# Attention loop ordered by a table of places, scores from 16-bit high and low halves

## The chip, the cores and the metric

One core of a Trainium2 chip runs the kernel. The number that counts is the device time of one execution in microseconds. The kernel before was timed three times: 1871.81, 1875.1 and 1884.6 us, median 1875.1.

## The reference, cut to what matters

The input is 16 images of 3 x 256 x 256. A template correlation turns each image into 256 tokens of 256 numbers; then come one attention block and one gated feed-forward block, each followed by a layer normalisation. The change lies in the attention block (and in the last microseconds of the token stage, where its weights are prepared):

```python
x = rmsnorm(tokens, norm_w)                    # tokens 256 x 256 per image
q = (x @ Wq)  -> 16 heads of 64 ; k, v = x @ Wkv -> 8 heads of 64
q, k = l2norm over 64, times (gamma + 1) * 8
sim = q k^T                                    # two query heads share one key head
sim = 50 * tanh(sim / 50) * 64 ** -0.5, causal mask, softmax
out = (sum over the two query heads of attn v) @ Wout
h = layernorm(tokens + out)
```

## The kernel before, in words

The program has three stages, one block after the other, with a barrier between them: the token stage (correlation, lines 123 to 591), the attention stage (694 to 1142) and the feed-forward stage (1167 to 1501). All orders are written by hand; each engine runs its own list strictly in order and waits on semaphores. Nothing is scheduled by a compiler.

**Attention stage.** The 16 images go in 4 groups of 4. Each engine emits a `FIRST` stretch (image 0 is prepared), a loop of three `BODY` stretches (one group each, and meanwhile the next group's tokens and first image are prepared) and a `FINAL` stretch (the last group). A stretch is a list of steps made by `first_order` and `attention_order`, and every engine walks the same list and issues its part of each step. The steps:

- `turn_h`: transposes of the normalised tokens `hn` on TensorE, split by ScalarE and VectorE into `ht_hi` and `ht_lo`.
- `make` 0 to 7: projection to q, k, v of one image, six matmuls of 512 columns per bank; ScalarE copies the bank to `raw` or `v`. After each third it also squares `raw` (L900). `make` 8 to 14: four transposes of the scaled `raw`; ScalarE copies queries to `qt` (L904), VectorE multiplies keys by the folded gamma into `kt` (L988).
- `sum`, `root`, `scale`: VectorE's l2 norm of q and k.
- `score` n (n = 0 to 31 in a group: image times key head): four float32 matmuls on 64 rows each, two of 256 and two of 128 columns, where the pair m = 0, 1 uses the lower and the upper 64 rows (L1102); then ScalarE's tanh (L911) and exp (L914) and GpSimd's causal mask (L838).
- `mix` n: six float32 matmuls of 65 columns (L1116), two heads behind `score` n; VectorE divides by the sum (L995, L998, L1002).
- `turn_o`, `project`: output transposes (L1125, copied by ScalarE at L921) and the projection with `w_out` (L1137), one `project` series of 64 matmul passes at the end of a group; VectorE adds it to `h` and takes the statistics.
- `rms_sum`, `rms_root`, `rms_scale`: the next group's tokens `hn` are squared and summed by ScalarE (L872), rooted by GpSimd (L829, L831), scaled by VectorE (L941). `rms_sum` stands behind score 17 of the group.

Three PSUM banks (`BANKS`) serve all of `turn_h`, `make`, `turn_o` and `project` in rotation: a step waits until the one three places earlier has been read out; the first of a stretch waits until all of the stretch before are (L1056). Scores have two buffers, `mixed` has one.

**The load of the next group's tokens.** SyncE's list for a group is: wait until all bank jobs of the stretch before are done, load `hn` (L785), then words and `h`, and at the end of the group wait for the normalised `h` (`s_x1`, set by VectorE's L1034) and store it (L805). So the load of `hn` for the next group stands behind the store of the group before.

## Time and profile before

| | |
|---|---|
| median of 3 runs | 1875.1 us (1871.81 to 1884.6) |
| the profiled execution, its own time | 1875.0 us |
| its span, first to last instruction | 1873.3 us |
| token stage | 0 to 523.5 us |
| attention: preparation and first group | 523.5 to 721.6 us |
| attention: second, third group | 721.6 to 885.4, 885.4 to 1049.1 us |
| attention: last group | 1049.1 to 1198.6 us |
| feed-forward stage | 1198.6 to 1873.3 us |
| mean granted TensorE clock | 0.980 of full |

The borders of groups are the first score matmul behind a projection. TensorE is at work 95% of the span, VectorE 59%, ScalarE 47%, GpSimd 23%. A duration of a single matmul in the trace holds the length of the pipe; what a matmul costs in a row of them is the distance from start to start.

### The profile page before, as it was taken

The numbers are of one execution on the slowest core, as the hardware profiler recorded it, in microseconds if no ns is written. First come the engines' busy times: TensorE is split into PE (matmuls) and PEld (weight loads), VectorE is DVE, ScalarE is ACT, GpSimd is POOL, SyncE is SP. The second block draws the span as 40 slices with busy tenths as digits, with TensorE's granted clock in tenths as the row PEclk, the third lists the DMA queues.
The fourth block names the chain that finished last, engine by engine and source line by source line (L and its number), as shares of the span: only waits on it lengthen the run. The fifth ranks groups of instructions, "written<-read, shape, count | busy, mean of one in ns | idle before, by whom it ended". The sixth has DMA issues, their size and how long they took to land. (4 is left out here: it accounts for less than half of the span.)

```text
span 1873.3 us, 31348 instructions
## 1 busy us (share of the span) xinstructions
PE 1781.0 (95%) x11640; PEld 1548.6 (83%) x11640; DVE 1104.9 (59%) x1964; ACT 873.9 (47%) x1077; POOL 429.0 (23%) x516
## 2 busy tenths in 40 slices
PE   5999999999969999999999999799999999999998
PEld 5999999999958877877787788688888888888886
DVE  9899898998756665565666656334141432415142
ACT  6555566665437764684676477122222222222221
POOL 2000000000212221211222123143343434434342
PEclk9999999999979999999999999799999999999999
DMA  5323212224010002000200102240000000000000
GB/s 175 120 90 124 82 74 83 82 78 155 23 70 34 24 17 85 24 16 10 92 24 17 61 25 95 72 153 23 0 24 1 23 24 1 23 1 23 1 12 12
DMA packets 26363, 97.11 MB, mean 52 GB/s; under 512 B 3033, under 2 KB 11353, under 8 KB 20962
## 3 DMA queue, kind: packets, MB, share of 16 engines
q1 hardware_dynamic: 26210, 94.96, 14.7%
q8 instruction: 110, 1.80, 0.4%
q14 instruction: 43, 0.35, 0.1%
HBM read 82.33 MB, written 24.15 MB: 57 GB/s over the span
## 5 line engine op out<-in xcount | busy, mean ns | idle before, releaser
L569 PE MATMUL conv<-w_hi,x_hi 128*128 128x368 f16 (+5 forms) x1320 | 353.0, 278 | 3.5 <-issue 3.5
L569 PE MATMUL conv<-w_lo,x_hi 128*128 128x368 f16 (+5 forms) x1320 | 353.8, 278 | 0.0
L569 PE MATMUL conv<-w_hi,x_lo 128*128 128x368 f16 (+5 forms) x1320 | 352.6, 278 | 0.0
L1328 ACT ACTIVATE raw_c<-ring,sh 128x512 f32<-128x512 f32 x128 | 87.5, 689 | 334.4 <-PE ring L1431 334.3
L838 POOL TENSOR_SCALAR_AFFINE_SELECT probs<-probs 128x256 f32<-128x256 f32 x256 | 124.4, 509 | 430.7 <-ACT probs L914 430.7
L1116 PE MATMUL mixed<-v,probs 128*128 128x65 f32 x1536 | 199.2, 280 | 14.7 <-DVE o L998 11.9
L1116 PEld LDWEIGHTS mixed<-v,probs 128*128 128x128 f32 x1536 | 182.9, 193 | 31.2 <-issue 16.0
L1287 POOL TENSOR_TENSOR ha_lo<-raw_c,ha_hi 128x512 fp32r<-128x512 f32 x128 | 165.3, 1291 | 189.3 <-DVE ha_hi L1340 189.3
L1340 DVE CAST ha_hi<-raw_c 128x512 fp32r<-128x512 f32 x128 | 86.3, 674 | 201.0 <-ACT raw_c L1328 198.8
L569 PEld LDWEIGHTS conv<-w_hi,x_hi 128*128 128x128 f16 x1320 | 192.3, 146 | 12.4 <-issue 4.0
L569 PEld LDWEIGHTS conv<-w_lo,x_hi 128*128 128x128 f16 x1320 | 192.6, 146 | 8.1
L1431 PE MATMUL ring<-ha_hi,wh 128*128 128x512 f32 x512 | 199.2, 389 | 0.0
L1431 PE MATMUL ring<-ha_lo,wh 128*128 128x512 f32 x512 | 199.2, 389 | 0.0
L1431 PE MATMUL ring<-hb_lo,wh 128*128 128x512 f32 x512 | 199.2, 389 | 0.0
L1431 PE MATMUL ring<-hb_hi,wh 128*128 128x512 f32 x512 | 199.2, 389 | 0.0
L569 PEld LDWEIGHTS conv<-w_hi,x_lo 128*128 128x128 f16 x1320 | 192.0, 145 | 7.5
L911 ACT ACTIVATE probs<-sim 128x768 f32<-128x768 f32 x128 | 103.8, 811 | 99.3 <-PE sim L1102 97.8
L1340 DVE CAST hb_hi<-raw_c 128x512 fp32r<-128x512 f32 x64 | 35.8, 559 | 187.7 <-ACT raw_c L1328 187.3
L326 ACT ACTIVATE lines<-turn 128x512 f32<-128x512 f32 x96 | 50.0, 606 | 172.1 <-PE turn L550 172.1
L1102 PE MATMUL sim<-qt,kt 64*128 64x256 f32 (+1 forms) x1024 | 120.0, 354 | 3.2 <-DVE kt L988 2.8
L1102 PEld LDWEIGHTS sim<-qt,kt 64*128 64x128 f32 x1024 | 89.9, 189 | 39.9 <-issue 33.0
L412 DVE TENSOR_TENSOR_SCAN box<-lines 128x271 f32<-128x271 f32 x192 | 120.1, 699 | 3.9 <-ACT lines L326 3.9
(148 smaller groups left out, 3443.4 us busy)
## 6 DMA issues: line engine op xcount, KB each, us to landing
xt<-x_columns_in SPq DMA_DIRECT2D x12, 1163.0 KB, 6.0
xp<-x_patches_in SPq DMA_DIRECT2D x12, 1152.0 KB, 5.1
hidden_words<-hidden_weights_in SPq DMA_DIRECT2D x8, 1408.0 KB, 8.0
words<-hidden_words SPq DMA_DIRECT2D x32, 352.0 KB, 3.1
wh<-hidden_words SPq DMA_DIRECT2D x8, 1024.0 KB, 10.0
tokens<-planes SPq DMA_DIRECT2D x4, 1024.0 KB, 4.6
lines<-tokens SPq DMA_DIRECT2D x4, 1024.0 KB, 5.6
h<-tokens SPq DMA_DIRECT2D x4, 1024.0 KB, 6.9
```

The source lines that it names most:

```text
L326: act.activation(dst, turn[:, k % 4], ACT.Copy).then_inc(s_across, 1)
L412: return dve.tensor_tensor_scan(out, line[:, TH:TH + SCAN], line[:, 0:SCAN], 0.0, ALU.add, ALU.subtract)
L569: ins = pe.matmul(out, xs[:, c, RI - 1 - i:RI - 1 - i + NR, :, x].rearrange("p r g -> p (r g)"), w, start=(t == 0), stop=(t == len(terms) ...
L838: ins = pool.affine_select(out=diag, in_=diag, compare_op=ALU.is_ge, fill=0.0, base=0, pattern=[[0, 2], [1, P]], channel_multiplier=-1)
L911: act.activation(probs[:, n % 4], sim[:, n % 2, :, 0:3 * P], ACT.Tanh, scale=1.0 / CLAMP).then_inc(s_tanh, 1)
L1102: ins = pe.matmul(sim[:, n % 2, m, 2 * P * jb:2 * P * jb + P * (2 - jb)], kt[rows, img % 2, hd, P * jb:P * jb + P], qt[rows, img % 2, hd, ...
L1116: ins = pe.matmul(out, probs[:, n % 4, m, at:at + P], v[:, img % 2, jb, 2 * (hd // 2) + m], start=(jb == 0), stop=(jb == ib), skip_group_c ...
L1287: pool.tensor_tensor(dst[1][:, u % KH], raw[:, u % 4], dst[0][:, u % KH].bitcast(F32), ALU.subtract).then_inc(s_lo, 1)
L1328: act.activation(raw[:, u % 4], bank, ACT.Gelu, scale=scale[:, m:m + 1]).then_inc(s_gelu, 1)
L1340: dve.tensor_copy(dst[0][:, u % KH], raw[:, u % 4]).then_inc(s_hi, 1)
L1431: ins = pe.matmul(bank, a, b, start=start, stop=False, skip_group_check=True)
```

## The change

**Places.** Each step gets a number of its own, in units of heads (`IMAGE_AT` for images 1 to 3 of a group, `EDGE_AT` for the next group's image 0, `GROUP_AT` for the steps of a group), and the list of a stretch is the steps sorted by it. The squaring becomes a step (`square`), the transposes are now `turn`, and `rms_sum` falls into four pieces of two squares each, written to a buffer of their own (`dump`). Sorted, three of the four pieces of `rms_sum` (places -28.062, -15.449, -0.477) come ahead of score 0 (place 0), which opened the list before, and ahead of the group's first `make`. The three banks stay.

**Scores.** q times the folded gamma is kept as a float16 high part (ScalarE, four activations of 128 columns with a scale read per partition) and a float16 rest (VectorE, four scalar_tensor_tensor); keys likewise, times 8, without gamma, once per pair of key heads (one activation, one scalar_tensor_tensor). A score is 12 float16 matmuls, three terms (hi hi, lo hi, hi lo) of what were 4 float32 ones. The gamma is brought into the range of float16 by a maximum over all partitions: GpSimd's `partition_all_reduce` at the end of its list in the token stage, and four small VectorE instructions behind it (`fold_span`), ahead of the stage's last `scale`. The tanh takes its scale from an SBUF column.

```diff
             split_weights()
+            pool.wait_ge(sh.s_gamma, 6)
+            pool.partition_all_reduce(sh.span[:, 1:2], sh.span[:, 0:1], P, bass.bass_isa.ReduceOp.max)\
+                .then_inc(sh.s_span, 1)
...
+            def fold_span():
+                dve.wait_ge(sh.s_span, 1)
+                dve.tensor_scalar(sh.span[:, 2:3], sh.span[:, 1:2], 1.0 / GAMMA_SPAN, 1.0, ALU.mult, ALU.max)\
...
                     scale_tokens()
+                    fold_span()
                 scale(g, c, n, 3)
...
-SLOTS = (
...
+IMAGE_AT = {
+    ("make", 1): -8, ("make", 2): -8, ("make", 0): -7.681, ("square", 0): -7.022, ("sum", 0): -6.626,
...
+GROUP_AT = {
+    ("rms_sum", 0): -28.062, ("rms_sum", 1): -15.449, ("rms_sum", 2): -0.477, ("rms_sum", 3): 15.005,
...
+    at += [(t, step) for step, t in GROUP_AT.items() if not last or step[0] == "project"]
+    return [step for t, step in sorted(at)]
...
                         act.wait_ge(s_hn, n * 16 + 16)
-                        if run.before:
-
-                            act.wait_ge(s_ss, image(g, RMS_AT // HEADS + 1) * 2 + 2)
-                        for a in range(PR):
-                            ins = act.activation(squares[:, a * D:(a + 1) * D], hn[:, a], ACT.Square,
-                                                 accum_out=ss[:, a:a + 1])
-                        ins.then_inc(s_hsum, 1)
+                        for a in range(2 * step[1], 2 * step[1] + 2):
+                            ins = act.activation(dump[:, a], hn[:, a], ACT.Square, accum_out=ss[:, a:a + 1])
+                        if step[1] == 3:
+                            ins.then_inc(s_hsum, 1)
...
+                        if r < 2:
+                            for e in range(4):
+                                u = 4 * r + e
+                                ins = act.activation(q_hi[:, img % 2, u, cols], bank[:, e * P:(e + 1) * P], ACT.Copy,
+                                                     scale=gamma[:, u:u + 1])
+                            ins.then_inc(s_qkhi, 1)
+                        else:
+                            act.activation(k_hi[:, img % 2, :, cols], bank.rearrange("p (h t) -> p h t", t=P),
+                                           ACT.Copy, scale=KEY_SCALE).then_inc(s_qkhi, 1)
...
-                                       scale=1.0 / CLAMP).then_inc(s_tanh, 1)
+                                       scale=sh.span[:, 2:3]).then_inc(s_tanh, 1)
...
+                                ins = dve.scalar_tensor_tensor(out=q_lo[:, img % 2, u, cols], in0=bank[:, e * P:(e + 1) * P],
...
                         for jb in range(2):
-                            for m in range(2):
-                                rows = slice(DH * m, DH * m + DH)
-                                ins = pe.matmul(sim[:, n % 2, m, 2 * P * jb:2 * P * jb + P * (2 - jb)],
-                                                kt[rows, img % 2, hd, P * jb:P * jb + P],
-                                                qt[rows, img % 2, hd, P * jb:TOK], start=True, stop=True)
+                            for t, (k, q) in enumerate(((k_hi, q_hi), (k_hi, q_lo), (k_lo, q_hi))):
+                                for m in range(2):
+                                    rows = slice(DH * m, DH * m + DH)
+                                    ins = pe.matmul(sim[:, n % 2, m, 2 * P * jb:2 * P * jb + P * (2 - jb)],
+                                                    k[rows, img % 2, hd // 2, P * jb:P * jb + P],
+                                                    q[rows, img % 2, hd, P * jb:TOK], start=(t == 0), stop=(t == 2),
+                                                    skip_group_check=True)
```

SyncE's list and GpSimd's masks are as they were.

What moves, at the three places that matter below. **ScalarE, around the start of the loop over groups** (`UNCONDITIONAL_BRANCH` and the `ISA` behind it enter the loop; `lines` holds `hn`, `b_hn` is the semaphore of its load, `b_job` that of a finished bank). Before:

```order
L904 ACTIVATE qt<-job 128x4x128 [waits b_score,b_job] x4
L689 UNCONDITIONAL_BRANCH
L689 ISA
L910 REGISTER_ALU [waits b_score]
L911 ACTIVATE probs<-sim 128x768 [waits b_mix]
L913 REGISTER_ALU
L914 ACTIVATE probs<-probs 128x768 [waits b_tanh]
L859 ISA
L888 ACTIVATE raw<-job 128x512 [waits b_job]
```

and now:

```order
L951 ACTIVATE k_hi<-job 128x4x128 [waits b_score,b_job]
L727 UNCONDITIONAL_BRANCH
L727 ISA
L911 ACTIVATE dump,ss<-lines 128x256 [waits b_hn]
L911 ACTIVATE dump,ss<-lines 128x256
...
L901 ISA
L926 ACTIVATE raw<-job 128x512 [waits b_job]
L901 REGISTER_ALU
L926 ACTIVATE raw<-job 128x512 [waits b_job]
L955 ISA
L956 REGISTER_ALU [waits b_score]
L957 ACTIVATE probs<-sim,span 128x768 [waits b_mix]
```

Six squares that wait for the load now open ScalarE's list of a group; the first two bank copies and the first tanh stand behind them.

**TensorE, at the same place** (`job` is a bank). Before, a score came first, then three `make` steps; now two `make` steps come first, then a score, a `make` and a score, and the fourth `make` waits for ScalarE's first bank copy (`b_emptied_act`). The score itself and its neighbours now:

```order
L1155 MATMUL sim<-q_hi,k_hi 128x256 [waits b_tanh]
L1155 MATMUL sim<-q_hi,k_hi 128x256
L1155 MATMUL sim<-q_lo,k_hi 128x256 x2
L1155 MATMUL sim<-q_hi,k_lo 128x256 x2
L1155 MATMUL sim<-q_hi,k_hi 128x128 x2
L1155 MATMUL sim<-q_lo,k_hi 128x128 x2
L1155 MATMUL sim<-q_hi,k_lo 128x128 x2
L1109 REGISTER_ALU
L1133 MATMUL job<-wqkv_hi,ht_hi 128x512 [waits b_emptied_act]
```

where before stood:

```order
L1102 MATMUL sim<-qt,kt 128x256 [waits b_tanh]
L1102 MATMUL sim<-qt,kt 128x256
L1102 MATMUL sim<-qt,kt 128x128 x2
L1055 REGISTER_ALU
L1082 MATMUL job<-wqkv_hi,ht_hi 128x512 [waits b_emptied_act]
```

Four matmuls became twelve; the wait of the next `make` is of the same kind.

**GpSimd, at the end of the token stage** (the bare `ISA` ahead of the maximum is the reload of the library):

```order
L286 TENSOR_TENSOR wqkv_lo<-xt_sq,wqkv_hi 128x1024 [waits b_whi] x2
L297 ISA
L297 ISA span<-span 128x1 [waits b_gamma]
L134 UNCONDITIONAL_BRANCH
L855 UNCONDITIONAL_BRANCH [waits barrier_Pool_Activation_PE_DVE_SP_gather]
```

and in the loop over groups, between two masks:

```order
L871 ISA [waits b_hsum]
L871 TENSOR_SCALAR rms<-ss 128x8
L873 TENSOR_TENSOR rms<-rms,neg_half 128x8 [waits b_hmean]
```

The first `ISA` and the maximum are new; the reload that goes back stands ahead of `rms_root`, inside the loop.

## Rows read from the trace of the kernel before

**Rows 1.** Stretches: us, then busy PE, PEld, DVE, ACT, POOL; clock, DMA share, GB/s.

```profile
721.60:885.40 163.80, 154.52 (x1041) 129.71 (x1040) 102.82 (x248) 105.17 (x148) 34.92 (x68) 0.98 0.12 38
```

**Rows 2.** TensorE's waits in that group (total us, times, longest).

```profile
PE mixed L1116 <- DVE o L998: 4.2, 5, 1.9
PE job L1082 <- DVE ht_lo L948: 1.7, 1, 1.7
```

**Rows 3.** Timeline, TensorE: a make's last matmuls, a score, a mix (start, duration).

```profile
606.29 0.39 PE L1082 MATMUL job<-wqkv_lo,ht_hi 128*128 128x512 f32 x1
606.52 0.40 PE L1082 MATMUL job<-wqkv_hi,ht_lo 128*128 128x512 f32 x1
606.85 0.92 PE L1102 MATMUL sim<-qt,kt 64*128 64x256 f32 x8
607.70 1.55 PE L1116 MATMUL mixed<-v,probs 128*128 128x65 f32 x12
```

**Rows 4.** Timeline: the projection at the first group's end and what follows it.

```profile
705.87 15.77 PE L1137 MATMUL job<-w_out,ot 128*128 128x256 f32 x64 [1.59 <-ACT ot L921]
721.57 0.92 PE L1102 MATMUL sim<-qt,kt 64*128 64x256 f32 x8
722.62 0.81 ACT L911 ACTIVATE probs<-sim 128x768 f32<-128x768 f32 x1 [16.80 <-PE sim L1102]
726.18 2.84 DVE L1034 TENSOR_SCALAR h<-h,moments_b,rstd_b 128x256 f32<-128x256 f32 x8 [2.24 <-POOL rstd_b L846]
729.20 0.90 SPq L805 DMA_DIRECT2D attended<-h  x2
730.80 0.35 SPq L785 DMA_DIRECT2D lines<-tokens  x1
```

**Rows 5.** The three loads of the next group's tokens, issue to landing.

```profile
DMA to landing us min/median/max: 5.0/6.2/6.6
```

**Rows 6.** Timeline, TensorE: float16 matmuls of the correlation, 120 and 248 columns.

```profile
100.08 0.23 PE L569 MATMUL conv<-w_hi,x_hi 128*128 128x120 f16 x1
...
100.59 0.23 PE L569 MATMUL conv<-w_hi,x_lo 128*128 128x120 f16 x1
...
101.14 0.27 PE L569 MATMUL conv<-w_hi,x_hi 128*128 128x248 f16 x1
101.25 0.27 PE L569 MATMUL conv<-w_lo,x_hi 128*128 128x248 f16 x1
```

**Rows 7.** Groups by line, ScalarE and VectorE (count, busy us, mean ns, idle before).

```profile
L888 ACT ACTIVATE raw<-job 128x512 f32<-128x512 f32 x24 | 14.1, 594 | 11.9 <-PE job L1082 11.9
L872 ACT ACTIVATE lines<-lines 128x256 f32<-128x256 f32 x8 | 3.2, 409 | 0.0
L337 ACT ACTIVATE guess<-std,eps_t 128x2048 f32<-128x2048 f32 x12 | 24.2, 2016 | 0.1
L339 ACT ACTIVATE guess<-guess 128x2048 f32<-128x2048 f32 x12 | 23.2, 1931 | 0.1
L998 DVE TENSOR_TENSOR o<-mixed,rl 128x256 f32<-128x256 f32 x16 | 6.8, 424 | 0.6
L988 DVE TENSOR_TENSOR kt<-job,gamma 128x512 f32<-128x512 f32 x16 | 10.2, 682 | 0.0
```

**Rows 8.** Timeline, GpSimd and VectorE at the end of the token stage.

```profile
512.37 5.62 POOL L282 TENSOR_TENSOR wqkv_lo<-xt_sq,wqkv_hi 128x1024 fp32r<-128x1024 f32 x2
521.29 0.68 DVE L473 SCALAR_TENSOR_TENSOR planes<-conv,planes 128x512 f32<-128x512 f32 x1
```

**Rows 9.** Timeline, around the library's two reloads at the attention stage's end.

```profile
1177.84 0.38 POOL L850 PARTITION_ALL_REDUCE lows<-lows  x1 [7.81 <-DVE lows L1014]
1198.68 1.07 PE L1419 MATMUL ring<-ident_c,x_c 128*128 128x128 f32 x8 [2.92 <-PEq L703]
1208.03 0.26 POOL L1279 TENSOR_SCALAR rstd_b<-moments_b 128x8 f32<-128x8 f32 x1 [29.81 <-issue]
```

**Rows 10.** Timeline: the first score of the first group, after image 0's preparation.

```profile
557.45 1.65 PE L1102 MATMUL sim<-qt,kt 64*128 64x256 f32 x8 [1.46 <-DVE kt L988]
```

More of the change, by code:

```diff
@@ L60, in __init__ @@
         self.gamma = sb("gamma", [P, HEADS])
+        self.span = sb("span", [P, 4])
         self.ss = sb("ss", [P, PR])
@@ L647 @@
-RMS_AT = 2 * HEADS + 1
+    order += [("make", 0, j) for j in (0, 1, 2)] + [("square", 0, 0), ("sum", 0, 0), ("root", 0, 0)]
+    order += [("make", 0, j) for j in (4, 5, 6)] + [("square", 0, 1), ("scale", 0, 0), ("sum", 0, 1), ("root", 0, 1)]
+    order += [("make", 0, j) for j in (3, 7)]
+    for tb in range(2):
+        order += [("scale", 0, 1)] if tb else []
+        for r in range(3):
+            order += [("turn", 0, 4 * tb + r)] + ([("low", 0, 4 * tb + r)] if ("low", r) in IMAGE_AT else [])
@@ new lines, in first_order @@
+    return order
+def attention_order(last):
+    at = []
+    for img in range(GI):
+        first = img * HEADS
+        for hd in range(HEADS):
+            at += [(first + hd, ("score", first + hd)), (first + hd + MIX_AT, ("mix", first + hd))]
+        at += [(first + HEADS - 1 + LAG + TURN_O_AT[b], ("turn_o", img, b)) for b in range(2)]
+        at += [(first + BITS_AT[b], ("bits", 2 * img + b)) for b in range(2)]
+        if img:
+            at += [(first + t, (kind, img, k)) for (kind, k), t in IMAGE_AT.items()]
+    if not last:
+        at += [(NH + t, (kind, GI, k)) for (kind, k), t in EDGE_AT.items()]
+    at += [(t, step) for step, t in GROUP_AT.items() if not last or step[0] == "project"]
+    return [step for t, step in sorted(at)]
@@ L653, in emptied_on @@
 def emptied_on(step):
-    if step[0] == "make" and step[2] >= 8:
+    if step[0] == "turn":
         return "queries" if step[2] % 4 < 2 else "keys"
@@ L724, in attention_stage @@
         ot = sb("ot", [P, EB, PR, NR, GI])
+        dump = sb("dump", [P, PR, D])
         stats = sb("stats", [P, PR, 6])
@@ L1072, in emit @@
                     elif kind == "make":
[L1073 to L1074 removed]
+                        img, tb, r = step[1], step[2] // 4, step[2] % 4
                         bank = free_bank(run, g, step)
[L1076 to L1091 removed]
@@ new lines, in emit @@
+                        if step == run.fresh:
+                            pe.wait_ge(s_emptied["dve"], run.emptied_before(g, "dve") + run.counts[run.jobs["turn_h", 3]][1])
+                        terms = [(f, x, w) for f in range(FB) for x, w in ((ht_hi, w_hi), (ht_hi, w_lo), (ht_lo, w_hi))]
+                        for t, (f, x, w) in enumerate(terms):
+                            ins = pe.matmul(bank, x[:, f, img % GI, P * tb:P * tb + P], w[:, f, 512 * r:512 * r + 512],
+                                            start=(t == 0), stop=(t == len(terms) - 1))
@@ new lines, in emit @@
+                        ins.then_inc(s_job, 1)
+                    elif kind == "turn":
+                        img, tb, r = step[1], step[2] // 4, step[2] % 4
+                        bank = free_bank(run, g, step)
+                        pe.wait_ge(s_qn, image(g, img) * 2 + tb + 1)
+                        for e in range(4):
+                            c = (4 * r + e) * P
+                            ins = pe.transpose(bank[:, e * P:(e + 1) * P], raw[:, tb, c:c + P], ident[:])
+                        ins.then_inc(s_job, 1)
```

200 lines of the change are left out of this document (99 added, 101 removed).

## The prediction

> **What bounds the kernel now.** I read the windows by stage first. The change touches the attention stage (523.5 to 1198.6 us) and the last microseconds of the token stage; the 675 us behind it stay. In a middle group TensorE is at work 154.5 of 163.8 us, ScalarE 105.2, VectorE 102.8 [rows 1]: TensorE sets the pace, and the others cost only where it waits for them. Its own waits are few: the largest is for VectorE's read of `mixed`, 4.2 us, the next for `ht_lo`, 1.7 us [rows 2]. So a change here is worth what it takes from TensorE's list, less what it makes TensorE wait for. The reader should then look at the border of two groups [rows 4]: TensorE goes from the projection straight to the next score at 721.57, ScalarE follows 1.05 us later after 16.8 us of rest, while VectorE normalises until 729.0, SyncE stores that and only then, at 730.80, issues the load of the next group's tokens. Nobody waits for this load before: its user stands behind score 17.
>
> The sum is made against the profiled execution, 1875.0 us (span 1873.3), which is the median of the runs within 0.1 us.
>
> **The scores.** A score takes 0.85 us from its start to the next step's [rows 3]. Its eight passes are 256 and 128 columns wide; the projection's 64 passes of 256 columns take 15.7 us, 0.245 each [rows 4], so one behind the other the eight would need 4 x 0.245 + 4 x 0.12 = 1.46 us. The two halves of the array therefore run side by side: 2 x 0.245 + 2 x 0.12 = 0.73 us, and 0.12 us are the start. The new score is twelve float16 matmuls, six pairs. Float16 with 248 columns comes every 0.11 us, with 120 columns every 0.064 us (eight distances between 100.08 and 100.59) [rows 6]. As pairs side by side: 3 x 0.113 + 3 x 0.066 + 0.12 = 0.66 us, a saving of 0.19. If no float16 matmul may start less than 0.064 us behind the last, half or not: 12 x 0.064 + 0.12 = 0.89 us, no saving. Not side by side at all would be 1.2 us, which the 0.85 of today excludes. I take 0.71, near the first, since the pairs of today are pairs on the same halves: 0.14 us each, times 128 scores, **-18 us** (0 to -24).
>
> The Trainium skill (TensorE: Matmul & The Clock Gate, section "Wait — 56ns, not 53.3ns?") names a floor per matmul of about 25 ns, and one of about 62 ns when the hardware decode is off. By the second figure the twelve need 0.74 us and the start, and this term is nearly nothing; the spacing of 0.064 us agrees with it but could as well be the weight load's.
>
> **The load at the head of ScalarE's list.** Three of the four `rms_sum` pieces now open a group's list, and wait for the load. Counted from the first TensorE step of the group (721.57 in [rows 4]): issue at +9.2 us, landing 6.2 us later [rows 5], six squares of 0.41 us [rows 7], then the first bank copy of 0.59: +18.5 us. The load cannot come earlier: its issue hangs on VectorE's normalisation and the store, which stay where they were. TensorE has work until its fourth `make`, which needs that copy: three `make` of six matmuls at 0.23 us [rows 3], 1.4 each, and two scores of 0.7, together 5.7 us. So 12.8 us are lost, and ScalarE, who then has two copies, a tanh, an exp and a square of `raw` to catch up, gives about 2 more: an estimate, the length of one square and one copy. Two borders have this in full, between groups 1 and 2 and 2 and 3; the last group has no `rms_sum`. 15 us each, **+30 us** (22 if the load lands in 5.0 us and nothing has to be caught up; 38 if four more are).
>
> **The head of the first group.** There the load can go out as soon as image 0's transposes are done, and TensorE starts later anyway. VectorE now makes three low parts ahead of `scale` 1, 8 x 0.295 + 0.68 = 3.0 us in place of 1.3 (0.295 us for 128 columns, from 424 ns for 256 and 682 for 512 [rows 7]); behind the last transposes come ScalarE's high and VectorE's low parts in a chain about 1.3 us longer than the two multiplications that released the score at 557.45 [rows 10]. The group's first `make` waits for all banks, thus for the last low part. **+3 us** (0 to 6); TensorE's 5.7 us of work then cover the landing.
>
> **The maximum over partitions.** GpSimd ends its split at 517.99; VectorE would reach `fold_span` at 521.29 [rows 8]. Between stands a reload of the library. Its price has two rows: after L850 the way back took from 1198.68, where the other engines began, to 1208.03, 9.35 us; ahead of L850 at most the 7.81 us of idle time that VectorE's result is named for [rows 9]. With 7 us, 0.4 for the maximum and about 0.9 for four instructions on a few columns (an estimate, half of the 0.42 for 256 columns each), VectorE resumes 5.0 us later, and the barrier with it: **+5 us** (0.9 if the reload is free, 7.4 if it takes 9.35). The engines have nothing left in that stage to hide it.
>
> The Trainium skill (GPSIMD Engine Reference, section 2.1 Instruction dispatch) puts the first call of a freshly loaded kernel at about 6 us. By that the term would be 4 us, and the next one would nearly vanish; the 9.35 us of the row are more, and I go by the row.
>
> **The way back** stands ahead of `rms_root` of the first group, between the masks of scores 15 and 16. A head lasts (163.8 - 15.7) / 32 = 4.6 us, a mask is needed two heads after its score. The mask of 16 would be ready some 3.7 us after its score; behind 9.35 us of reload, which starts about when the mask of 15 ends, it comes some 3 us after its `mix`: **+3 us**, once (0 to 7).
>
> **The places.** What they can give is TensorE's waits inside a group. `turn_h` now stands well ahead of the `make` that waited 1.7 us, and the long VectorE instructions are spread between the `mix` reads that cost 4.2 [rows 2]. I take two thirds of 5.9, for three groups: **-12 us** (-18 to 0).
>
> **At nothing** I cost what falls on the other engines. VectorE gets 16 x 4 x 0.295 + 8 x 0.68 - 10.2 = 14 us per group onto 102.8; ScalarE 32 tanh with a scale from memory at 0.085 (2016 - 1931 ns [rows 7]), the queries at up to 1.0 more for each of 16, and eight key activations of 0.59: at most 2.7 + 16 + 4.8 = 23.5 onto 105.2. Their rest of about 60 us hides both; if it is gone, the second rival's price holds. The buffers `dump`, the moved `norm` and the smaller tiles cost nothing.
>
> **Sum:** -18 + 30 + 3 + 5 + 3 - 12 = +11, **1886 us**, 0.6% over the median. A difference under 1% (18.7 us) can't be told from none here.
>
> **Rivals.**
> 1. *The twelve matmuls are bound by their issue*, one per 0.064 us whatever the half. For it: the even 0.064 us at 120 columns [rows 6]. Against it: pairs of today that overlap. The first term is gone: 1886 + 18 = **1904 us**. It decides from 0.064 us per matmul on. This is the page's second floor as a mechanism of this kernel.
> 2. *ScalarE becomes the bound of the loop.* Its group would hold 105.2 + 23.5 = 129 us of work, and at the border it rests the 16.8 us of the projection and the 15.4 until the load lands, less 3 us of copies: 158 of a group that I put at 163.8 - 4.5 + 15 - 4 = 170. So 12 us remain for waits on TensorE, where today there are about 42 outside the border. If 20 must stay, a group lasts 178, 8 more, three times: **1910 us**. It decides from more than 12 us of such waits. Against it: tanh and exp have two heads of lead.
> 3. *The wait at the head costs TensorE nothing*, and the move of `rms_sum` does what a step ahead of its time should do. It needs the load before TensorE's 5.7 us are over. For it: the pieces were put apart from the scores, so ScalarE is freer in mid group; against it SyncE's order [rows 4]. Then 1886 - 30 = 1856, with the full saving of the scores **1850 us**.
>
> **How the numbers follow.** Forecast 0.54, rivals 0.14, 0.18 and 0.14. The predicted time is the forecast's. The range 1862 to 1908 takes in the bounds of its terms (load 8 us either way, reloads, scores) and rival 1, and leaves out rival 3 and the upper half of rival 2. Slower by over 1%, above 1894 us: rivals 1 and 2 and a small part of the forecast's own upper edge, 0.36. Faster by over 1%, below 1856 us: most of rival 3, 0.10. Within 1%: 0.54.
>
> **What the profile of the changed kernel would show.** At the borders of groups: ScalarE's first square waiting for the load, and a hole of about 13 us in TensorE behind its third `make`, at the second and third group, with the granted clock at its lower level (1.2 GHz) for some microseconds after it. A score start to start near 0.71 us; 0.89 is rival 1. The maximum's row near 525 us, attention's first transposes near 529.6 in place of 524.6. A gap of some 10 us between two masks in the first group. The waits of `mix` on VectorE under 2 us a group. The prediction is wrong if there is no hole behind the third `make`, if the holes spread through the group behind bank copies and tanh (rival 2), or if the groups shrink below 160 us.

## The result, and the profile after

The changed kernel takes 1906.1 us (median of four runs, 1903.2 to 1911.0), the kernel before 1873.5 in the same job: a ratio of 1.016 over all runs, 95% interval 1.012 to 1.021. It is slower; 1886 us were forecast, 20 less, with a range of 1862 to 1908 that holds the result near its end. The spans differ by 28.2 us, 1901.5 against 1873.3, and nearly all of it lies in the attention stage.

The first view to read is again the one by stretches. Its first three rows answer to [rows 1], where the second group of the kernel before took 163.80 us; the fourth is the last group. The border of the second and third group before, given as 885.4, is 885.76 by the first score, so these two took 164.19 and 163.35 us; the first took 164.12. The stretches run from the first TensorE step of a group's list to that of the next.

```profile
563.04:724.03 160.99, 149.18 (x1168) 123.65 (x1168) 111.66 (x289) 119.76 (x204) 29.73 (x66) 0.97 0.10 31
724.03:890.50 166.47, 147.29 (x1169) 121.83 (x1169) 113.94 (x303) 119.54 (x204) 31.26 (x68) 0.96 0.12 38
890.50:1058.20 167.70, 147.17 (x1168) 121.81 (x1169) 114.76 (x305) 119.38 (x204) 31.46 (x68) 0.95 0.11 37
1058.20:1226.77 168.57, 149.00 (x1081) 125.50 (x1081) 94.62 (x261) 100.75 (x156) 30.81 (x67) 0.85 0.15 50
```

The last group of the kernel before, in the same view:

```profile
1049.11:1198.68 149.57, 140.40 (x953) 119.26 (x953) 86.92 (x220) 88.84 (x114) 34.25 (x67) 0.95 0.17 56
```

Taken in order, the first step of the groups' list comes 5.6 us later than the first score before (563.04 against 557.45 [rows 10]), the first group is 3.1 us shorter, the second and third are 2.3 and 4.4 us longer, the last is **19.0** us longer, and the rest of the program differs by 0.1. Two things are to be seen. In the second and third group TensorE works 7 us less than before and rests 10 and 12 us more. In the last group, which has no next tokens to load, it works 8.6 us *more* although each of its 32 scores is 0.25 us shorter (below): its clock is 0.85 in place of 0.95.

**The border of two groups**, as a timeline of ScalarE, VectorE, SyncE's queue and TensorE; it answers to [rows 4].

```profile
731.33 0.35 SPq L827 DMA_DIRECT2D lines<-tokens  x1
732.07 0.60 SPq L833 DMA_DIRECT2D words<-hidden_words  x1
...
737.39 0.42 ACT L911 ACTIVATE dump<-lines 128x256 f32<-128x256 f32 x1 [24.82 <-DMA lines<-tokens]
...
738.36 0.89 DVE L1061 TENSOR_TENSOR bits<-bits,words 128x704 int32<-128x704 int32 x1 [8.82 <-DMA words<-hidden_words]
...
739.80 1.06 ACT L926 ACTIVATE raw<-job 128x512 f32<-128x512 f32 x2
740.43 0.79 PE L1133 MATMUL job<-wqkv_hi,ht_hi 128*128 128x512 f32 x1 [10.53 <-ACT raw L926]
```

This is the forecast hole: the load lands at 737.39, six squares later comes the bank copy, and TensorE, out of work at 729.90, goes on at 740.43. At the next border the hole is 11.6 us. But there is a second wait beside it that was not forecast: VectorE's `bits` waits 8.82 us for the load of `words` that stands behind the tokens in SyncE's queue, and ends 1 us after the first.

**TensorE's and VectorE's groups by line** (count, busy us, mean ns, then idle before it and what ended it) for the attention stage; the first answers to [rows 2].

```profile
L1170 PE MATMUL mixed<-v,probs 128*128 128x65 f32 x1536 | 210.4, 290 | 27.6 <-DVE o L1052 24.1 <-DVE parts L1052 3.4
L1133 PE MATMUL job<-wqkv_hi,ht_hi 128*128 128x512 f32 x240 | 106.9, 445 | 28.0 <-ACT raw L926 22.1 <-DVE h L1072 2.7 <-DVE k_lo L1041 2.4
...
L1061 DVE TENSOR_TENSOR bits<-bits,words 128x704 int32<-128x704 int32 x32 | 31.7, 991 | 66.4 <-DMA words<-hidden_words 66.4
```

The last row is the one to stop at. In the kernel before it reads:

```profile
L1007 DVE TENSOR_TENSOR bits<-bits,words 128x704 int32<-128x704 int32 x32 | 30.7, 958 | 3.6 <-DMA words<-hidden_words 3.6
```

VectorE's rest for `words` went from 3.6 to 66.4 us. The places of `bits` are 0.042 and 7.9 of each image, so the second of one image and the first of the next stand 0.14 heads apart, and there is one `words` buffer: its next load goes out when the first of the two is done. What that does in the last group, as a timeline (SyncE's row holds two loads):

```profile
1162.13 1.08 DVE L1061 TENSOR_TENSOR bits<-bits,words 128x704 int32<-128x704 int32 x1
1163.25 4.49 SPq L833 DMA_DIRECT2D words<-hidden_words  x2
...
1166.35 1.03 DVE L1061 TENSOR_TENSOR bits<-bits,words 128x704 int32<-128x704 int32 x1 [3.13 <-DMA words<-hidden_words]
...
1167.51 0.42 DVE L1052 TENSOR_TENSOR o<-mixed,rl 128x256 f32<-128x256 f32 x1
1168.08 2.79 PE L1170 MATMUL mixed<-v,probs 128*128 128x65 f32 x12 [4.19 <-DVE o L1052]
```

The read of `mixed` stands behind `bits` in VectorE's list, and TensorE's next `mix` behind that read: 4.19 us of rest. The `mix` then takes 2.79 us in place of 1.55. By stretches, what follows:

```profile
1167.90:1212.30 44.40, 39.85 (x208) 34.84 (x209) 9.75 (x27) 14.43 (x16) 4.99 (x13) 0.50 0.23 83
1212.30:1223.80 11.50, 11.50 (x54) 9.83 (x52) 4.33 (x9) 0.00 (x0) 0.00 (x0) 1.00 0.00 0
```

For 44.4 us, through all the heads that are left and 5 us into the projection, the granted clock is 0.50, the lower level of 1.2 GHz, though TensorE works 39.85 of them. It all begins with one wait for 704 columns of words; `last_bits`, below, prices it.

**A score**, as a timeline of TensorE; it answers to [rows 3].

```profile
1158.17 0.28 PE L1155 MATMUL sim<-q_hi,k_hi 64*128 64x256 f16 x2
1158.29 0.27 PE L1155 MATMUL sim<-q_lo,k_hi 64*128 64x256 f16 x2
...
1158.77 0.44 PE L1170 MATMUL mixed<-v,probs 128*128 128x65 f32 x2
```

From its start to the next step it takes 0.60 us, where it took 0.85 and 0.71 were forecast. **The two reloads of GpSimd's library**, which answer to [rows 8, 9]:

```profile
522.42 0.38 POOL L297 PARTITION_ALL_REDUCE span<-span  x1 [5.53 <-issue]
522.84 0.15 DVE L512 TENSOR_SCALAR span<-span 128x1 f32<-128x1 f32 x1 [2.56 <-POOL span L297]
...
526.87 2.79 PE L1124 MATMUL job<-ident,lines 128*128 128x128 f32 x12 [8.48 <-PEq L134]
...
636.39 0.19 POOL L871 TENSOR_SCALAR rms<-ss 128x8 f32<-128x8 f32 x1 [6.83 <-issue]
```

In front of these two rows nothing but the reload stands in GpSimd's list: the way there took 5.53 us, the way back 6.83, between two masks of the first group. The Trainium skill (GPSIMD Engine Reference, section 2.1 Instruction dispatch) puts the load that the first call of a freshly loaded kernel pays at 5.95 us; these rows lie on either side of it, and nearer to it than the 7 and 9.35 us that the prediction took from [rows 9].

### The profile page after: what moved, and what is told of

Its sections match the earlier page's. It is cut to its first block and busy times, and to the rows that moved or that the text cites. A ratio compares the mean times of both kernels' runs of the same rounds, so it can differ in the third digit from the quotient of the medians.

```text
span 1901.5 us, 33002 instructions
## 1 busy us (share of the span) xinstructions
PE 1768.2 (93%) x12152; PEld 1531.5 (81%) x12152; DVE 1152.1 (61%) x2195; ACT 932.7 (49%) x1301; POOL 417.3 (22%) x517
## 5 line engine op out<-in xcount | busy, mean ns | idle before, releaser
L1170 PE MATMUL mixed<-v,probs 128*128 128x65 f32 x1536 | 210.4, 290 | 27.6 <-DVE o L1052 24.1
L1170 PEld LDWEIGHTS mixed<-v,probs 128*128 128x128 f32 x1536 | 196.3, 204 | 42.1 <-issue 24.9
L880 POOL TENSOR_SCALAR_AFFINE_SELECT probs<-probs 128x256 f32<-128x256 f32 x256 | 110.7, 457 | 460.2 <-ACT probs L960 460.2
L1133 PE MATMUL job<-wqkv_hi,ht_hi 128*128 128x512 f32 x256 | 114.5, 447 | 30.7 <-ACT raw L926 22.1
L957 ACT ACTIVATE probs<-sim,span 128x768 f32<-128x768 f32 x128 | 115.3, 901 | 18.4 <-PE sim L1155 18.0
L1485 PEld LDWEIGHTS ring<-ha_hi,wh 128*128 128x128 f32 x512 | 96.1, 188 | 21.6 <-POOL ha_lo L1341 1.6
```

The source lines that it names most:

```text
L880: ins = pool.affine_select(out=diag, in_=diag, compare_op=ALU.is_ge, fill=0.0, base=0, pattern=[[0, 2], [1, P]], channel_multiplier=-1)
L957: act.activation(probs[:, n % 4], sim[:, n % 2, :, 0:3 * P], ACT.Tanh, scale=sh.span[:, 2:3]).then_inc(s_tanh, 1)
L1133: ins = pe.matmul(bank, x[:, f, img % GI, P * tb:P * tb + P], w[:, f, 512 * r:512 * r + 512], start=(t == 0), stop=(t == len(terms) - 1))
L1170: ins = pe.matmul(out, probs[:, n % 4, m, at:at + P], v[:, img % 2, jb, 2 * (hd // 2) + m], start=(jb == 0), stop=(jb == ib), skip_group_c ...
L1485: ins = pe.matmul(bank, a, b, start=start, stop=False, skip_group_check=True)
```

## The experiments

Three theories stood against each other after this reading: the load at the head of ScalarE's list (the forecast one); the waits for `words`, with the clock that falls behind them; and, for the clock, the float16 scores themselves. Each edit is on the changed kernel where nothing else is said.

### The two moved steps, apart and together

```diff
-    ("rms_sum", 0): -28.062, ("rms_sum", 1): -15.449, ("rms_sum", 2): -0.477, ("rms_sum", 3): 15.005,
+    ("rms_sum", 0): 6.9, ("rms_sum", 1): 7.4, ("rms_sum", 2): 14.95, ("rms_sum", 3): 15.005,
```

> The changed kernel with its first three rms_sum pieces at places 6.9, 7.4 and 14.95 of the group in place of -28.062, -15.449 and -0.477; nothing else differs. Theory A (the load at the head of ScalarE's list): in the trace of the changed kernel TensorE rests 10.53 us at 729.9 and 11.55 us at 896.4 until ScalarE's copy of raw, and the clock is at 1.2 GHz for 10.2 and 13.7 us behind them, of which about half is lost. Both holes go: 22 us, and about 6 more by the clock, 1906 - 28 = 1878 us. Rival A2 (the holes were hidden behind what the group waits for later, on VectorE): the groups keep their 166 us, 1906 us. Rival A3 (the squares, put among the tanh and exp of the later heads, make their own waits): half is given back, about 1892 us, and waits of mix on the mask appear near places 7 and 15.

Measured: 1900.1 us, ratio to the kernel before 1.014 (1.010 to 1.019). Only 6 us came back, less than theory A's 28 and than A3's 14. The timeline at the same border says why:

```profile
735.06 0.35 SPq L827 DMA_DIRECT2D lines<-tokens  x1
735.80 0.60 SPq L833 DMA_DIRECT2D words<-hidden_words  x1
...
742.19 0.89 DVE L1061 TENSOR_TENSOR bits<-bits,words 128x704 int32<-128x704 int32 x1 [8.91 <-DMA words<-hidden_words]
...
747.83 0.45 PE L1170 MATMUL mixed<-v,probs 128*128 128x65 f32 x1 [6.99 <-DVE o L1052]
```

ScalarE waits for the load no more, and TensorE's hole is still 7 us: now it is `mix` that waits, for VectorE, which waits for words. Two waits for loads that land within 1 us of each other cover each other, and taking one away shows the other.

```diff
-MIX_AT, TURN_O_AT, BITS_AT = LAG + 0.105, (1.076, 1.326), (0.042, 7.9)
+MIX_AT, TURN_O_AT, BITS_AT = LAG + 0.105, (1.076, 1.326), (2.042, 6.042)
```

> The changed kernel with its bits steps at places 2.042 and 6.042 of each image in place of 0.042 and 7.9; nothing else differs. Theory B: VectorE's bits rests 66.4 us for the load of words in the changed kernel (3.6 before), 16 times, because the second of two neighbouring bits comes 0.14 heads after the first and the load between them takes over 3 us. Behind these rests TensorE's mix waits (4.94 us at 1071.1, 4.19 us at 1163.9, some 2 us in other images), and the 4.19 us near the end are followed by 44 us at 1.2 GHz. Spread evenly, the rests fall to under 10 us. If the hole of 4.19 us is what takes the clock down and keeps it down through the last heads, these heads take 2.1 us each in place of 3.83 (7 of them, 12 us), and with the holes and their clock (about 22 us) the time is 1906 - 34 = 1872 us. Rival B2 (the clock stays low in the last heads because of the float16 scores, whether there is a hole or not): 1906 - 22 = 1884 us, with the half clock still there from about 1165 on. Rival B3 (the rests of VectorE are hidden): 1906 us.

Measured: 1890.2 us, ratio 1.010 (1.003 to 1.017). VectorE's rest for words fell from 66.4 to 0.1 us, and the last group from 168.6 to 144.6 in the profiles, 5.0 under the kernel before, where the forecast had 4.5. One of the four runs took 1906.7 at a mean clock of 0.958, so the low clock can come without these waits too. At the borders the squares' hole stayed, 13.2 and 11.4 us, and the total gained 16 us, not 34.

> Both of the edits of squares_late and bits_even on the changed kernel. If both theories hold and neither hides the other: 1906 - 28 - 34 = 1844 us, 1.6% under the kernel before. If one hole lay in the shadow of the other (the words for the first bits are loaded behind the tokens in the same queue): about 1855 us. If the low clock in the last heads comes from the float16 scores themselves: about 1856 us, with half clock in the last 40 us of the stage.

Measured: 1868.2 us, ratio 0.999 (0.996 to 1.001). Both edits give 38 us, where each alone gave 6 and 16: the remaining 16 could be had only by taking both waits away. What is left at the border, and in the first group:

```profile
742.48 0.89 DVE L1061 TENSOR_TENSOR bits<-bits,words 128x704 int32<-128x704 int32 x1 [3.08 <-DMA words<-hidden_words]
...
744.07 0.76 PE L1170 MATMUL mixed<-v,probs 128*128 128x65 f32 x4 [4.13 <-DVE o L1052]
...
637.36 0.20 POOL L871 TENSOR_SCALAR rms<-ss 128x8 f32<-128x8 f32 x1 [7.55 <-issue]
...
639.37 3.08 DVE L987 TENSOR_SCALAR lines<-lines,rms 128x256 f32<-128x256 f32 x8 [6.71 <-POOL rms L873]
...
643.61 0.66 PE L1179 MATMUL job<-ident,o 128*128 128x128 f32 x2 [4.47 <-DVE o L1056]
```

### One hole alone, and the same hole in the kernel before

```diff
-        at += [(first + BITS_AT[b], ("bits", 2 * img + b)) for b in range(2)]
+        moved = 2 if last and img == GI - 1 else 0
+        at += [(first + BITS_AT[b] + (moved if b == 0 else 0), ("bits", 2 * img + b)) for b in range(2)]
```

> The changed kernel, with one step moved: in the last group the first bits of its last image stands at 26.042 in place of 24.042, two heads behind its neighbour at 23.9. It prices one hole alone, the 4.19 us at 1163.9 and what the clock does behind it. Theory A: the hole takes the clock to 1.2 GHz, and in heads that are score and mix alone it doesn't come back, so the hole costs its 4 us and about 12 for seven heads at 3.83 us in place of some 2.1: the last group goes from 166.5 to about 150, the time to 1890 us. Rival A2: another wait a head or two later takes the clock down as well, and only the hole itself is won: 1901 us.

Measured: 1892.5 us, ratio 1.010 (1.007 to 1.012), 14 us less and nearer to theory A (1890) than to A2 (1901). The last group, by stretches:

```profile
1064.30:1215.50 151.20, 134.23 (x1080) 112.56 (x1080) 94.77 (x261) 100.51 (x156) 30.97 (x67) 0.94 0.17 56
```

168.6 us became 151.2 in the profile by moving one instruction two heads. The other way round, in the kernel before:

```diff
-        if n % (NH // CHUNKS) == 2 and n < NH:
+        if n % (NH // CHUNKS) == 2 and n < NH and not (last and n == NH - 2):
             order.append(("bits", n // (NH // CHUNKS)))
+            if last and n == NH - 6:
+                order.append(("bits", n // (NH // CHUNKS) + 1))
```

> The kernel before, with the last two bits of its last group side by side behind head 26 (before: behind 26 and 30), so that VectorE waits for a load of words in the last image there too. The rest, float32 scores included, is as before. Theory A: the hole of some 3.5 us takes the clock down for the five heads that are left and until the projection has run some 4 us, as in the changed kernel: 3.5 + 5 x 1.7 = 12 us more, 1885 us, half clock from about 1158 to 1187. Rival A2 (only float16 scores leave the clock low): 3.5 us more, 1877 us, and half clock for under 15 us behind the hole. Rival A3 (the wait is hidden): 1873 us.

Measured: 1887.1 us, ratio 1.007 (1.004 to 1.010), against 1885 by theory A and 1877 by A2. The wait, the hole and the stretch behind it:

```profile
1162.51 0.89 DVE L1009 TENSOR_TENSOR bits<-bits,words 128x704 int32<-128x704 int32 x1 [3.39 <-DMA words<-hidden_words]
...
1164.10 1.30 PE L1118 MATMUL mixed<-v,probs 128*128 128x65 f32 x5 [3.34 <-POOL probs L840]
...
1162.80:1196.90 34.10, 28.65 (x117) 25.20 (x118) 7.78 (x21) 6.90 (x8) 3.90 (x9) 0.50 0.22 83
```

The hole's releaser is named as GpSimd's mask there, but VectorE's row ahead of it shows what came first. Float32 scores, an old order, one hole of 3.3 us: the clock is low for 34 us, to 5 us into the projection. So the float16 scores are not needed for it. Not all of the 34 us are the hole's doing, though: in the kernel before, without it, the clock falls at the last two `mix` of the group, behind rests of 0.83 us, and is back 4 us into the projection:

```profile
1169.90:1183.90 14.00, 10.67 (x40) 9.18 (x40) 2.96 (x7) 1.94 (x2) 0.50 (x2) 0.51 0.01 1
```

The hole brings the fall some 20 us forward here.

### The scores alone

```diff
-        q_hi = sb("q_hi", [P, 2, HEADS, TOK], F16)
+        q_hi = sb("q_hi", [P, 2, HEADS, TOK])
...
-                            for t, (k, q) in enumerate(((k_hi, q_hi), (k_hi, q_lo), (k_lo, q_hi))):
+                            for t, (k, q) in enumerate(((k_hi, q_hi),)):
```

(`k_hi` likewise; `q_lo` and `k_lo` keep one buffer in place of two.)

> The changed kernel, places and all, but its high parts are float32 and its score is the eight float32 matmuls of before; the low parts are still made on VectorE and not used, so that the other engines keep their work. It tells the float16 score apart from the rest. A score takes 0.60 us from its start to the next step's in the changed kernel, 0.85 in the kernel before. If TensorE sets the pace throughout: 128 x 0.25 = 32 us more, 1938 us. If the waits on VectorE and ScalarE take up part of it (the holes at the borders and the rests for words shrink as TensorE comes later): 1920 us. On the clock: if the float16 scores keep it at 1.2 GHz in the last heads, the half clock behind the hole near the end lasts under 15 us here, as it did in the kernel before, and the time is nearer 1915 us; if the hole does it, it lasts 40 us or more.

Measured: 1923.0 us, ratio 1.025 (1.021 to 1.029): 17 us more than the changed kernel, below the 32 of a bound TensorE. On the clock its profile, of the longest of five runs (1935.5 us), agrees with the last section:

```profile
1198.10:1242.50 44.40, 40.24 (x177) 35.37 (x176) 9.72 (x26) 14.43 (x16) 5.00 (x13) 0.50 0.22 81
```

> The kernel with both steps moved (both_moved), with the float32 score in place of the float16 one; the low parts are made and not used, as in scores_f32. There the float32 score cost 17 us where 128 x 0.25 = 32 were expected. If the holes of the changed kernel took up the rest, and TensorE sets the pace once they are small: 32 us over both_moved, 1900 us. If VectorE and ScalarE set the pace for half of the heads anyway: 17 us over it, 1885 us. Against the kernel before, whose scores are the same, the difference is what places, low parts and token stage cost together: 27 us or 12 us.

Measured: 1886.2 us, ratio 1.006 (1.004 to 1.008): 18 us over `both_moved`, again not 32. So it isn't the holes that take up the rest. The second group of both kernels, float16 first:

```profile
726.95:884.50 157.55, 146.70 (x1169) 122.16 (x1169) 114.62 (x305) 118.43 (x204) 31.80 (x68) 0.98 0.12 40
```

```profile
735.20:897.70 162.50, 154.72 (x1041) 129.49 (x1041) 114.12 (x303) 119.39 (x204) 31.20 (x68) 0.98 0.12 39
```

TensorE's work falls by 8.0 us, which is 32 x 0.25, and the group by 4.95: 3.1 us turn into rests, 1.8 of them in `mix` waiting for VectorE's reads (5.9 in place of 4.1 us). Against the kernel before, which has the same scores, `both_f32` is 12 us slower: what places, low parts and token stage cost once the two steps stand better. By the borders in the two profiles all of it lies ahead of the second group, which begins at 735.2 in place of 721.6; the three groups from there on are together 4.2 us shorter than before.

### Taking the rest away

```diff
+            pool.wait_ge(sh.s_span, 1)
+            pool.tensor_scalar(sh.span[:, 0:1], sh.neg_half[:, 0:1], 1.0, 1.0, ALU.mult, ALU.add).then_inc(sh.s_span, 1)
...
-MIX_AT, TURN_O_AT, BITS_AT = LAG + 0.105, (1.076, 1.326), (2.042, 6.042)
+MIX_AT, TURN_O_AT, BITS_AT = LAG + 0.105, (1.076, 1.326), (3.042, 7.042)
```

> both_moved with two further edits. The bits steps stand at 3.042 and 7.042 of each image, a head later, since in both_moved the first of a group still waits 3.08 us for words that are loaded behind the next tokens, and mix of TensorE 4.1 us behind it, at two borders. And GpSimd does one small tensor_scalar right behind the partition maximum, so that the library comes back while the attention stage starts, and not ahead of rms_root between two masks, where GpSimd stood idle 7.55 us, VectorE waited 6.71 for rms, and TensorE 4.5 at 639.1. Expected: two holes of 4 us and about 2 us of low clock each gone, 10 to 12 us; the hole at 639.1 down to the 1 us of the other groups and its low clock with it, 5 us: 1868 - 16 = 1852 us. If the library is fetched again ahead of rms_root all the same (the masks in between bring it out again): 1857 us. If the waits for words only move to the next head: 1864 us.

Measured: 1878.0 us, ratio 1.003 (1.001 to 1.005), 10 us worse than `both_moved` where 16 better were expected. The expectation overlooked that all engines meet GpSimd at the end of the token stage:

```profile
525.52 0.38 POOL L297 PARTITION_ALL_REDUCE span<-span  x1 [5.68 <-issue]
...
533.35 0.18 POOL L300 TENSOR_SCALAR span<-neg_half 128x1 f32<-128x1 f32 x1 [7.45 <-issue]
...
534.18 1.09 PE L1126 MATMUL job<-ident,lines 128*128 128x128 f32 x4 [12.86 <-PEq L134]
...
1152.00:1196.40 44.40, 40.03 (x209) 34.89 (x210) 10.51 (x27) 15.85 (x18) 5.73 (x15) 0.50 0.22 83
```

The reload went from one place where it was waited for to another: TensorE's rest there rose from 8.5 to 12.9 us. The last row is a second surprise: the clock is low in the last heads again, with no rest of over 0.8 us in the 10 us ahead of it. Of its ten runs six took 1873 to 1879 us at a mean clock of 0.965 to 0.972, and four 1887 to 1889 at 0.960 to 0.962; the profile is of one of the four.

```diff
-        at += [(first + BITS_AT[b], ("bits", 2 * img + b)) for b in range(2)]
+        at += [(first + BITS_AT[b] + (1 if img + b == 0 else 0), ("bits", 2 * img + b)) for b in range(2)]
```

> both_moved with the first bits of each group alone a head later (3.042 in place of 2.042); all other bits stay. In both_moved that first bits waits 3.08 us for words, and TensorE 4.13 and 3.9 us behind it at 739.9 and 897.4, with 6.8 us at 1.2 GHz after each. If these holes go and nothing takes their place: 2 x (4 + 3) = 14 us less at most, 1856 us. If it goes as in back_early, where all bits stood a head later and new holes of 1.7 to 1.9 us came with half clock behind them: 1868 us.

Measured: 1866.3 us, ratio 0.994 (0.992 to 0.996), 2 us under `both_moved`, which is within the spread of their runs; the two holes shrank from 4.1 and 3.9 to 3.1 and 2.4 us, and did not go.

The next one is `first_bits` with the maximum moved to the start (the two gamma loads behind SyncE's first bands, VectorE's six steps in `first`, GpSimd's maximum and a `tensor_scalar` behind its constants, `fold_span` in `fold_weights`):

```diff
             pool.memset(sh.neg_half[:], -0.5).then_inc(s_const, 1)
+            pool.wait_ge(sh.s_gamma, 6)
+            pool.partition_all_reduce(sh.span[:, 1:2], sh.span[:, 0:1], P, bass.bass_isa.ReduceOp.max)\
+                .then_inc(sh.s_span, 1)
...
                     scale_tokens()
-                    fold_span()
```

> first_bits, with the maximum over partitions at the start of the program: the two gamma loads, VectorE's six small steps on them and GpSimd's maximum stand at about 25 us, where GpSimd has nothing to do until 498, with one small tensor_scalar behind it that brings the library back there; VectorE's four steps on the result stand ahead of its 5 us of rest at 492. In back_early the library came back at the end of the token stage, where all engines wait for GpSimd: it took 7.45 us there, and the transposes began at 534.2. Expected: the transposes at 524.6 as in the kernel before (2.3 us won), no reload between the masks of the first group, its hole at 639.1 down from 4.5 to 1 us with the low clock behind it (5 us), 1 us lost at the start: 6 us under first_bits. If the library is fetched again in the first group: 2 us under it.

Measured: 1857.1 us, ratio 0.991 (0.988 to 0.994), 9 us under `first_bits` (6 expected) by the medians, though the intervals touch. TensorE's rest ahead of the first transposes is 5.1 us in place of 8.8, its hole of 4.2 us in the first group is gone, and from the first score to the first projection's end it is 149.3 us in place of 157.7. So the way back, which the prediction had at 3 us, cost about 8 in these profiles, with the low clock behind its hole. The maximum, and the last group, in which the low clock appeared in this profile:

```profile
29.00 0.82 POOL L284 PARTITION_ALL_REDUCE span<-span  x1 [15.46 <-DVE span L515]
...
1031.30:1187.30 156.00, 145.99 (x1080) 122.77 (x1081) 92.78 (x261) 100.12 (x156) 29.26 (x67) 0.86 0.16 54
1128.00:1164.00 36.00, 34.14 (x203) 30.12 (x202) 8.77 (x24) 14.64 (x17) 6.14 (x16) 0.50 0.29 102
```

```diff
-    order += [("make", 0, j) for j in (3, 7)]
+    order += [("make", 0, j) for j in (3, 7)] + [("scale", 0, 1)]
     for tb in range(2):
-        order += [("scale", 0, 1)] if tb else []
```

> max_early, with one step of the first image moved: VectorE does scale of its second tile ahead of the three low parts of its first (2.15 and 0.68 us, from 553.29 to 555.96), so that TensorE's last transposes of that image need not wait for them. In the changed kernel TensorE rests 6.87 us there and the last transposes start at 557.86, where the kernel before had its first score at 557.45. If the low parts are all that is ahead of them: the hole shrinks by 2.7 us and the first score comes 2 to 3 us earlier: 2.5 us under max_early. If the low parts of the second tile, now later in VectorE's list, are what the first make waits for: no change.

Measured: 1862.5 us, ratio 0.993 (0.990 to 0.996), not under `max_early`; the intervals overlap. In the profile the step does what was expected: TensorE's hole ahead of the last transposes is 5.3 us in place of 6.9, and from the first transposes to the first score it is 38.4 us in place of 40.8. Over the whole kernel 2.4 us don't stand out from what the last heads do from run to run, and the case stays open.

```diff
-                            for t, (k, q) in enumerate(((k_hi, q_hi), (k_hi, q_lo), (k_lo, q_hi))):
+                            more = 2 if run is FINAL and img == GI - 1 and jb == 0 else 0
+                            passes = [(k_hi, q_hi), (k_hi, q_lo)][:more] + [(k_hi, q_hi), (k_hi, q_lo), (k_lo, q_hi)]
+                            for t, (k, q) in enumerate(passes):
...
-                                                    q[rows, img % 2, hd, P * jb:TOK], start=(t == 0), stop=(t == 2),
+                                                    q[rows, img % 2, hd, P * jb:TOK], start=(t in (0, more)), stop=(t == more + 2),
```

> max_early, with work of no use added: in the last image of the last group each score does its first two passes of the 256-column half twice (the first time is overwritten), 0.22 us more per head. There TensorE's list holds scores and mixes alone, a head lasts 2.35 us by the way from mix over VectorE's read to the next mix with either kind of score, and TensorE rests 0.23 us in each with float16 (none with float32). In max_early the clock fell at 1127.6 with no rest above 1 us ahead of it, and stayed at 1.2 GHz for 44.4 us; that makes the last group 154.0 us in place of 142.5. If a fuller list keeps the clock at 2.4 GHz there: last group 143 us in most runs, no half clock before the last two mixes, median 1850 us. If it makes no odds what fills the list there: the profile again shows some 44 us, and the median stays at 1857 us. If the added passes lengthen the heads: 8 x 0.22 = 2 us more, 1859 us.

Measured: 1850.7 us, ratio 0.988 (0.985 to 0.991), the lowest median here, 1.2% under the kernel before; six runs from 1847.2 to 1855.2, where `max_early` went from 1848.4 to 1868.9. The two intervals overlap. The last group and the stretch in which the clock had fallen:

```profile
1030.20:1175.00 144.80, 134.50 (x1112) 112.85 (x1112) 93.27 (x261) 99.84 (x156) 29.87 (x67) 0.95 0.17 58
1115.00:1146.00 31.00, 28.35 (x326) 25.11 (x323) 19.08 (x52) 25.21 (x39) 10.08 (x24) 1.00 0.37 131
```

Matmuls whose result is thrown away cost nothing that can be seen: the last group is as long as in `bits_even` (144.6 us, without them), so they fit in rests that TensorE has there anyway. In this profile the clock stayed at 2.4 GHz through these heads. But it did so without added passes too, in the profiles of `bits_even`, `both_moved` and `first_bits`, and the profiled run here is the fastest of its six. That the passes hold the clock is suggested by the narrower spread and not shown.

## Why the prediction's range held and its sum did not

The direction and the range held, the range by luck: the outcome, slower by over 1%, had a chance of 0.36, and it came by a loss in the last group that stands in no term. By groups, with what lies ahead of the first put to it, the forecast of +11 us was +2.5, +6.5, +6.5 and -4.5, and the spans show +2.5, +2.3, +4.4 and +19.0. The first three lost less than forecast, 9 us in place of 15.5, and the last group used that up.

- **The scores, -18.** The size is right, the way to it is not. A score got 0.25 us shorter, not 0.14, which would be 32 us; the two float32 experiments give 17 and 18. What the prediction left out is that a shorter score lets TensorE arrive earlier at waits, those of `mix` on VectorE above all. Rival 1 (one matmul per 0.064 us) is refuted: twelve matmuls and the start take 0.60 us, less than 12 x 0.064 = 0.77. The Trainium skill (TensorE: Matmul & The Clock Gate, section "Wait — 56ns, not 53.3ns?") names about 62 ns per matmul as the bound with hardware decode off; by that figure twelve would need an estimated 0.74 us, and the rows don't agree with it. Which way matmuls are decoded here no run shows.
- **The load at the head of ScalarE's list, +30.** The mechanism is as told: first square waiting, hole behind the third `make`, half clock behind that. 12.8 us were forecast, 10.5 and 11.6 came, since SyncE issued the load 7.3 us after the group's first TensorE step and not 9.2. Rival 3 is refuted by these rows. But as a price the step is not 30: taken away alone it gives 6, because the words behind the same load hold VectorE as long, and 22 once `bits` stands elsewhere (1890.2 to 1868.2).
- **The head of the first group, +3.** Mis-sized. The first score came at 567.9 in place of 557.5; less two `make` that now stand ahead of it (2.8) and the later start (2.3), 5.3 us are left, the `make` at half clock among them.
- **The maximum, +5, and the way back, +3.** The first measured 3.3 by TensorE's rest ahead of the first transposes (8.5 us, 5.2 before), as the reload took 5.5 us and not 7; their start moved by 2.3 alone, from 524.61 to 526.87, since GpSimd's split ended 1.1 us earlier in this profile. The second showed a hole of 1.9 us in the changed kernel; with the two steps corrected it was 4.5, and moving both reloads away gave 9 us together by the medians, where 8 had been forecast.
- **The places, -12.** This is the step that failed. The sign given for it failed as well: `mix` waited 4.5 us for VectorE in the second group, not under 2. It looked at which waits of TensorE new places could take away, and not at what each moved step waits for. `bits` was moved as well, onto its neighbour, and its load with it: -12 became a loss, 16 us as measured alone and 32 once the squares stand elsewhere (1900.1 to 1868.2). 17 us of the last group's 19 hang on a single instruction, as the profile of `last_bits` shows (14 by the medians). No term and no rival had the clock of a stretch without `make` in it; the clock of 0.51 from 1169.9 to 1183.9 us, from the last two `mix` of the kernel before into its projection, was there to be read.
- **Rival 2 (ScalarE as the bound).** Its time, 1910 us, is 4 us from the measured one and rival 1's, 1904, only 2, which speaks for neither, since the mechanism of rival 1 is refuted above and that of rival 2 is not what happened: TensorE's largest waits are the two border holes on ScalarE, which are the forecast's, and those of `mix` on VectorE.

## What to carry to other kernels

A step that is given a new place takes its load, its buffer and its in-order neighbours with it: list for each moved step what it waits for, and how far it then stands from the step that frees that buffer. Two waits that end within a microsecond of each other hide each other, so take them away together before judging either. Ask of each hole what the engine has to do behind it: 4 us of rest cost 14 to 17 ahead of a list that was scores and mixes alone, since the clock stayed down for all of it.

## What the runs showed of the hardware

- TensorE's clock, once down to 1.2 GHz in the last heads (scores and `mix` alone), stayed there although TensorE worked 39.85 of 44.4 us, with float16 scores, and 40.24 with float32 scores, and came back 3 to 6 us into the projection in each profile. It fell behind holes of 3.3 to 4.2 us in the four profiles that have one there, but in three others (`back_early`, `max_early`, `scale_first`) as early with no rest above 1.0 us in the 25 us ahead of it, and in all the rest at the last two `mix`, behind rests of 0.83 us. So a hole is not needed for the early fall; what else sets it off stays open.
- The two halves of the array take a pair of float16 matmuls nearly at once: twelve of them, six pairs on 64 rows each, and the next step 0.60 us after the first.
- A GpSimd library came in 5.5 to 5.8 us and went back in 6.8 to 7.7 in the changed kernel and its variants, each time it was in the way; at 29 us in the program, with GpSimd at rest, it cost nothing that the profile shows.
